# The gated unit's candidate left in PSUM in an eight-unit block pipeline, with every step placed anew

## The reference

```python
x = x + mamba(layernorm(x))        # inner 256, 16 states, 4 taps; adds its own input again
x = x + ffn(layernorm(x))          # ternary weights, 128 -> 512 -> 128, exact gelu       ("a")
x = x + gated_unit(layernorm(x))   # minGRU, 512 features
x = x + ffn(layernorm(x))          # the same ternary ffn                                   ("d")

def gated_unit(x):
    x_in, x_skip = silu(x @ W1 + b1), silu(x @ W2 + b2)
    z = sigmoid(x_in @ Wz + bz)
    h_tilde = x_in @ Wh + bh
    # h[t] = (1 - z[t]) * h[t-1] + z[t] * h_tilde[t]
    h = associative_scan(combine, (1 - z, z * h_tilde))
    return (x_skip + h) @ Wo + bo
```

## Time and profile before

| | |
|---|---|
| median of three runs | 849.96 us (849.71 to 850.46) |
| the profiled execution | 846.95 us, of which span 844.40 us |
| TensorE busy | 702.1 us (83%) |
| VectorE busy | 677.2 us (80%) |
| ScalarE busy | 641.2 us (76%) |
| GpSimd busy | 588.8 us (70%) |
| granted TensorE clock, mean of the span | 0.921 of 2.4 GHz |
| state scans (line 1118), 256 | 298.2 us, mean 1206 ns |
| gated scans (line 1224), 32 | 51.8 us, mean 1636 ns |
| candidates (line 1216), 32 | 21.5 us, mean 670 ns |

### The profile page before, as it was taken

One profiled execution on the slowest core, in us unless ns is written; L12 is line 12 of the kernel. 1 busy time (PEld: TensorE's weight loads), 2 busy tenths in 40 slices (PEclk: granted clock), 3 DMA queues, 4 the chain that ended last, 5 costly groups with the idle time before them and its releaser, 6 DMA issues. The chain is left out here.

```text
span 844.4 us, 12621 instructions
## 1 busy us (share of the span) xinstructions
PE 702.1 (83%) x4116; PEld 593.8 (70%) x4116; DVE 677.2 (80%) x1063; ACT 641.2 (76%) x968; POOL 588.8 (70%) x375
## 2 busy tenths in 40 slices
PE   5655576799788997899789979899799968997995
PEld 5444365588677886688667867688678957786795
DVE  5699988889987998899987998899779988652131
ACT  5787867796889879997899778988898578525403
POOL 4399868777778687878786877968786667515302
PEclk9677776999899999999999999999899989997999
DMA  5511212111112211121111211121111111000000
GB/s 135 180 61 56 73 52 63 52 48 54 38 53 58 68 38 50 40 77 51 50 40 63 63 39 52 43 71 38 50 43 62 49 50 38 1 1 2 13 1 12
DMA packets 35185, 42.79 MB, mean 51 GB/s; under 512 B 7457, under 2 KB 17074, under 8 KB 35122
## 3 DMA queue, kind: packets, MB, share of 16 engines
q1 hardware_dynamic: 35122, 42.00, 16.4%
HBM read 39.63 MB, written 2.36 MB: 50 GB/s over the span
## 5 line engine op out<-in xcount | busy, mean ns | idle before, releaser
L514 POOL TENSOR_TENSOR inflow<-dtu,b_all 128x1024 f32<-128x1024 f32 x127 | 307.9, 2430 | 62.2 <-DVE state L1118 43.8
L1118 DVE TENSOR_TENSOR_SCAN state<-dA,inflow 128x512 f32<-128x512 f32 x256 | 298.2, 1206 | 24.0 <-ACT dA L865 23.7
L865 ACT ACTIVATE dA<-dt,decay_c 128x512 f32<-128x512 f32 x256 | 170.0, 686 | 62.3 <-DVE state L1118 61.2
L1135 DVE TENSOR_TENSOR state<-state,c_ps 128x1024 f32<-128x1024 f32 x128 | 155.4, 1214 | 18.1 <-PE c_ps L1425 13.5
L1434 PE MATMUL y_ps<-ident,state 128*128 128x128 f32 x1024 | 148.1, 293 | 0.0
L1434 PEld LDWEIGHTS y_ps<-ident,state 128*128 128x128 f32 x1024 | 132.4, 152 | 13.2 <-issue 2.7
L1425 PE MATMUL c_ps<-xd,pick 128*128 128x512 f32 x128 | 63.1, 493 | 77.4 <-DVE state L1135 77.1
L1316 PE MATMUL work<-in_hi,wzh_hi 128*128 128x512 f32 x256 | 104.5, 408 | 0.2 <-POOL in_lo L676 0.2
L1317 PE MATMUL work<-in_hi,wzh_lo 128*128 128x512 f32 x256 | 101.0, 395 | 0.0
L1318 PE MATMUL work<-in_lo,wzh_hi 128*128 128x512 f32 x256 | 101.0, 394 | 0.0
L1425 PEld LDWEIGHTS c_ps<-xd,pick 128*128 128x128 f32 x128 | 25.4, 199 | 97.8 <-DVE state L1135 93.3
(11 more groups left out here) (171 smaller groups left out, 1506.2 us busy)
## 6 DMA issues: line engine op xcount, KB each, us to landing
b_all<-b_scratch SPq DMA_DIRECT2D x128, 256.0 KB, 3.1
x_tok<-in_x SPq DMA_DIRECT2D x8, 256.0 KB, 3.8
out_x<-x_tok SPq DMA_DIRECT2D x8, 256.0 KB, 3.6
wide<-in_Wz SPq DMA_DIRECT2D x1, 1024.0 KB, 7.7
wide<-in_Wh SPq DMA_DIRECT2D x1, 1024.0 KB, 8.8
skip_f<-in_W SPq DMA_DIRECT2D x2, 256.0 KB, 4.3
dtu<-in_W_in SPq DMA_DIRECT2D x1, 256.0 KB
mixed<-in_w_up SPq DMA_DIRECT2D x1, 256.0 KB, 2.8
```

Of the source, the lines that this page charges most:

```text
L514: eng.tensor_tensor(inflow[:, n % 2, :, tok(b)], dtu[:, :, tok(b)], b_all[:, n % RING, tok(b)].unsqueeze(1).broadcast_to([P, HALVES, TO[b] ...
L865: act.activation(dA[:, h, tok(b)], dt[:, b % 2, h, tok(b)], ACT.Exp, scale=decay_c[:, h, n:n + 1]).then_inc(s_dA[h], 1)
L1118: dve.tensor_tensor_scan(state[:, g % 3, h, tok(b)], dA[:, h, tok(b)], inflow[:, n % 2, h, tok(b)], first, ALU.mult, ALU.add).then_inc(s_s ...
L1135: dve.tensor_tensor(state[:, g % 3, :, tok(b)], state[:, g % 3, :, tok(b)], c_ps[:, tok(b)].unsqueeze(1).broadcast_to([P, HALVES, TO[b] - ...
```

## The change

The candidate stays in the bank of `h<j>`, where it overwrites its product, and the gated scan reads it there, with `keep` from SBUF; its result goes to `mixed` as before. The bank is emptied by the scan, not by the candidate. The semaphore of the scans, `s_hid`, is gone, since `evacuated(..., "h<j>")` now says the same; the candidate gets one, `s_new`, for which the scan and ScalarE's next gate in that buffer wait. The waits for the readers of `mixed` move from the candidate to the scan.

Beside this all tables are new: the places on all four engines, `MOVED` (now for units 0 to 7), and `BANK`. Most places shift by a quarter or two of a step. The larger moves in the tables of all units are shown below; `x2b` goes from 26.75 to 32, `new2`, `hid2`, `new3` and `hid3` from 34.75, 36, 35.5 and 36.5 to one quarter, 35, and in the head `w12` from 1.25 to -9.25 and `sums` from -14.25 to -6.5. Within one quarter the list of VectorE has, for each j, `new<j>` and then `hid<j>`.

```diff
 POOL_AT = {
...
-    "d.sum1": 41.5, "d.sum2": 41.75, "d.sum3": 42, "d.rms": 42.75, "x2b": 26.75, "in_lo0": 27.25,
-    "in_lo1": 27.25, "in_lo2": 27.5, "in_lo3": 27.75, "keep0": 30, "keep1": 30.5, "keep2": 33, "keep3": 33.75,
...
+    "a.rms": 24.75, "d.sum1": 41.25, "d.sum2": 41.5, "d.sum3": 41.75, "d.rms": 42.5, "x2b": 32, "in_lo0": 27,
+    "in_lo1": 27.25, "in_lo2": 27.75, "in_lo3": 28, "keep0": 29.75, "keep1": 30.75, "keep2": 32.25, "keep3": 34,
...
 DVE_AT = {
...
-    "lo1": 19.75, "lo2": 27, "lo3": 39.75, "new0": 31, "hid0": 31.75, "new1": 33, "hid1": 34, "new2": 34.75,
-    "hid2": 36, "new3": 35.5, "hid3": 36.5, "sums": -14.25, "thr": -3, "signs0": 5.25, "signs1": 6.75,
...
+    "lo3": 39.25, "new0": 31, "hid0": 31.75, "new1": 32.5, "hid1": 32.75, "new2": 35, "hid2": 35, "new3": 35,
+    "hid3": 35, "sums": -6.5, "thr": -2, "signs0": 4.75, "signs1": 6.25, "bo_add": 2.25,
...
             def gru_keep(t, j):
 
                 evacuated(pool, t, "z%d" % j)
-                wait(pool, s_hid, FB * t + j - 1)
+                evacuated(pool, t if j >= 2 else t - 1, "h%d" % ((j + 2) % FB))
...
                 p = "z%d" % j
                 act.wait_ge(s_bzh, 2)
-                if j >= 2:
-                    evacuated(act, t, "h%d" % (j - 2))
-                else:
-                    evacuated(act, t - 1, "h%d" % (j + 2))
+                wait(act, s_new, FB * t + j - 1)
                 wait(act, s_keep, FB * t + j - 1)
...
                 p = "h%d" % j
                 full(dve, t, p)
                 evacuated(dve, t, "z%d" % j)
+                dve.scalar_tensor_tensor(bank(p)[:, tok(t)], gate[:, j % 2, tok(t)], 1.0, bank(p)[:, tok(t)],
+                                         ALU.add, ALU.mult).then_inc(s_new, 1)
+
+            def gru_scan(t, j, r, s):
+                p = "h%d" % j
+                dve.wait_ge(s_new, FB * t + j + 1)
+                dve.wait_ge(s_bzh, 2)
+                dve.wait_ge(s_keep, FB * t + j + 1)
                 read_by(dve, r, s, "out+")
                 evacuated(dve, 0, "down_t")
-                dve.scalar_tensor_tensor(mixed[:, j, tok(t)], gate[:, j % 2, tok(t)], 1.0, bank(p)[:, tok(t)],
-                                         ALU.add, ALU.mult).then_inc(*emptied(p))
-
-            def gru_scan(t, j):
-                evacuated(dve, t, "h%d" % j)
-                dve.wait_ge(s_bzh, 2)
-                dve.wait_ge(s_keep, FB * t + j + 1)
                 first = nbh_c[:, j:j + 1] if FROM[t] == 0 else mixed[:, j, FROM[t] - 1:FROM[t]]
-                dve.tensor_tensor_scan(mixed[:, j, tok(t)], keep[:, j % 2, tok(t)], mixed[:, j, tok(t)], first,
-                                       ALU.mult, ALU.add).then_inc(s_hid, 1)
+                dve.tensor_tensor_scan(mixed[:, j, tok(t)], keep[:, j % 2, tok(t)], bank(p)[:, tok(t)], first,
+                                       ALU.mult, ALU.add).then_inc(*emptied(p))
...
             def gru_out(t, k):
-                pe.wait_ge(s_hid, FB * t + k + 1)
+                evacuated(pe, t, "h%d" % k)
```

More of the change, by code:

```diff
@@ new lines @@
+    ("ACT", "z_copy1", 1): -10, ("DVE", "a.ms", 1): 24.25, ("DVE", "apply", 1): -17.25,
+    ("DVE", "d.ms", 1): 43.25, ("DVE", "d.out", 1): 43.25, ("DVE", "dtu", 1): -1.25, ("DVE", "dt", 1): -2,
+    ("DVE", "factors2", 1): 26.25, ("DVE", "factors3", 1): 38, ("DVE", "gate", 1): 16.5,
+    ("DVE", "hid0", 1): 31.5, ("DVE", "hid2", 1): 34.75, ("DVE", "hid3", 1): 36.25, ("DVE", "lo1", 1): 20,
+    ("DVE", "lo2", 1): 27.5, ("DVE", "lo3", 1): 39.75, ("DVE", "new0", 1): 30.5, ("DVE", "new1", 1): 32.25,
@@ new lines @@
+    ("DVE", "lo1", 6): 19.25, ("DVE", "lo3", 6): 42.25, ("DVE", "new1", 6): 31, ("DVE", "new3", 6): 35.75,
+    ("DVE", "norm", 6): -27.25, ("DVE", "read", 6): 0.25, ("DVE", "stats2", 6): 25.25,
[12 rows of a table added]
+    ("POOL", "base", 6): -4.75, ("POOL", "conv2", 6): -13.5, ("POOL", "conv3", 6): -11.5,
+    ("POOL", "d.rms", 6): 42.25, ("POOL", "d.sum2", 6): 41.25, ("POOL", "d.sum3", 6): 42,
+    ("POOL", "h_lo", 6): -15.25, ("POOL", "in_lo0", 6): 26.5, ("POOL", "in_lo1", 6): 26.5,
[9 rows of a table added]
+    ("ACT", "gated1", 7): 15, ("ACT", "h_tok", 7): -17.75, ("ACT", "hi1", 7): 16.25, ("ACT", "hi2", 7): 25.75,
@@ L232 @@
+    ("DVE", "x3", 7): 43.25, ("DVE", "xd_lo", 7): -5.5, ("PE", "a.down+", 7): 22.5, ("PE", "a.down", 7): 22.25,
[15 rows of a table added]
+    ("POOL", "base", 7): -2.25, ("POOL", "conv2", 7): -12.5, ("POOL", "conv3", 7): -12.25,
+    ("POOL", "d.rms", 7): 47.5, ("POOL", "d.sum1", 7): 46, ("POOL", "d.sum2", 7): 46,
[3 rows of a table added]
+    ("POOL", "root", 7): -20.75, ("POOL", "x2b", 7): 41.75,
 }
@@ L1299, in _ @@
                     for t in due(r, s, DVE_ON["hid%d" % j]):
-                        gru_scan(t, j)
+                        gru_scan(t, j, r, s)
         @block.tensor
```

115 lines of the change are left out of this document (59 added, 56 removed), and 229 rows, old and new, of tables (ACT_AT, BANK, DVE_AT, MOVED).

## The result

The changed kernel takes 854.56 us (median of 5 runs, 854.28 to 854.87) against 849.96 (5 runs, 847.45 to 850.82). The ratio is 1.0054, with a 95% interval of 1.0038 to 1.0071. Forecast were 847.2 us; 854.56 lies in the range of 836 to 859, but on the other side of "no change", where the second rival (the order costs more than the stalls did, 855) had put it.

What follows compares the result with a forecast made beforehand. No engine alone was taken to bound the passes (VectorE, TensorE, ScalarE all nearly full), TensorE the tail. Terms +1.5 - 1.8 - 0.6 - 0.4 - 1.5 = -2.8 us gave 847.2 us, range 836 to 859.

Steps and rivals of the forecast that it cites:

- the second rival: Scans forced ahead of fifth state scan and norm1's transposes cost more than the stalls did: 855 us, chance 0.30.
- Part 1, the stretch goes: Gated scans on VectorE, passes of units 2 to 7: stretching vanishes, 11.5 us of VectorE time, 1.9 us a pass.
- The new scan at 1.20 us: Gated scan reading PSUM takes 1.20 us instead of 1.28, like the state scan: 2.5 us more off VectorE.
- Part 1, the mechanism: A VectorE instruction with two SBUF operands and a GpSimd one block each other; six such pairs, one per pass.
- Part 2, the candidate: Writing the 32 candidates to PSUM on VectorE costs -0.5 to +1.8 us in all; 0 taken.
- Part 3: VectorE's candidate and scan become adjacent, pairs from 4 to 19; lost overlap 0.14 us, 15 times: 2.1 us.
- Part 4: VectorE's gated scans of blocks 2 and 3 ahead of fifth state scan, units 2 to 4; with part 1: +1.5 us.
- Part 5, rden_d: GpSimd's bias add moves later, so VectorE's rden_d no longer blocks: 6.1 us freed, 1.8 us taken as arriving.
- Part 6, "passes 0 and 1 get the same work: 0": First two passes have unchanged work, so the change in their time was taken as 0.
- Part 6, the tail: TensorE's work after the last state scan, in another order: 0.6 us off, ends -3 and +3.
- The 1.5 us for GpSimd's shorter waits: GpSimd waits less for gated scans and in_lo comes earlier: -1.5 us, ends 0 and -4.
- The sign that the prediction gave for it: Passes of units 4 to 6 above 93 us would show that the order costs more.

Runs made afterwards that it cites:

- e14_units234_up1: Changed kernel with signs1/split12 later, blocks 2 and 3 of units 2 to 4 re-placed (hid3 behind fifth state scan), unit 5's a.up1 at 20.25: 848.85 us, 0.9991.
- e5_hid3_behind: Changed kernel with new2, hid2, new3, hid3 of units 2 to 4 re-placed so block 3's scan stands behind the fifth state scan: 855.70 us, 1.0068.
- e13s_units23_signs: Changed kernel with signs1 and split12 later, and block 3's scan behind the fifth state scan in units 2 and 3 only: 849.02 us, 0.9987.
- e3_signs_moved: Changed kernel with signs1 on VectorE moved from 6.25 to 6.75 and split12 on GpSimd from 7.25 to 8.25: 853.06 us, 1.0033.
- e10_block1_behind: Changed kernel with block 1 of units 2 to 4 back at its old place (new1 33, hid1 34), z3, h3, gate3 moved for the bank: 856.48 us, 1.0075.
- e15_psum_blocks23: Kernel before with hid2 at 35.5, hid3 at 36, and the candidate in PSUM for blocks 2 and 3 alone: 863.96 us, 1.0158.
- e1c_block1_only: Kernel before with only hid1 of units 0 to 5 moved from 34 to 33: 868.26 us, 1.0214.
- e2_sbuf_new_tables: Changed kernel with all its tables, but the old data path (candidate in SBUF, scan reads it there): 869.76 us, 1.0229.
- e1b_order_only: Kernel before, candidate and scan in SBUF, with only VectorE's places moved as the bank would force them: 870.69 us, 1.0250.
- e1_psum_old_tables: Kernel before with VectorE's places moved as the bank would force them, plus the change's four code hunks (candidate in PSUM): 867.27 us, 1.0201.

## Why the prediction was wrong, step by step

- **Part 1, the stretch goes: right. The new scan at 1.20 us: wrong**, it is 1.28 as before. The prediction took the state scan as its model and overlooked that it starts from an immediate (0.0, in `mix_scan`) and the gated scan from a column, which makes up 0.060 of the 0.08 us. The 2.5 us from this did not come, nor did the 2.1 us of the page's rule: by the Trainium skill, "VectorE: DVE Perf Modes", the section on the TRN2 errata, a PSUM source costs 120 cycles of fixed cost and an SBUF source 58, an estimate of 65 ns more for the new scan. The medians are 1277 from SBUF and 1279 from PSUM.
- **Part 1, the mechanism: right.** A VectorE instruction with two SBUF operands is stretched beside GpSimd's work, 3.02 us for 1.28 and 2.27 for 0.16; with one operand in PSUM, the 32 gated scans and the 8 extra ones of each of two kernels never are. It is also what the Trainium skill states in "SBUF — State Buffer", section "Who interferes with whom" (the two share a pair of ports, which is held exclusively for a whole instruction). `m_vv` and `rden_d` (up to 1.88 and 2.35 us) show it for an instruction of one SBUF operand and constants too, the signs' comparison for one with a column in SBUF beside it. The prediction used this only for the instructions that it knew to be stretched. It never asked on which ones GpSimd's work would fall in the new order.
- **Part 2, the candidate: right**, 688 ns against 662, 0.8 us in all, inside its bounds.
- **Part 3:** in the trace the adjacent pairs go from 5 to 19, not from 4, which changes the term by 0.1 us. Candidate and scan stand 0.71 and 0.70 us apart (395.14 and 397.05 above), where 0.72 was taken.
- **Part 4 is the step that failed, by its size.** It took 1.3 us more in each of three passes, and 0.8 us less in each of three others: +1.5. In the profiles the passes of units 4, 5 and 6 are 4.2, 1.9 and 1.4 us longer, those of units 2, 3 and 7 change by -1.5, +0.1 and -0.6: +5.5. The second half was nearly right (-2.0 for -2.4), the first measures 7.5 for 3.9. The path that it drew is there: in the pass of unit 4 the transposes wait for the normalisation and come 1.8 us later. What it had no term for came on top. In the pass of unit 5 TensorE stands 2.35 us on a bank that only the scan frees, and 1.7 us come back where block 3's scan stands behind the fifth state scan. In the pass of unit 4 TensorE's clock is at 1.2 GHz for 10.2 us instead of 3.4, and the prediction counted all of TensorE's work at one speed. How much of the excess the order causes and how much the clock would have taken anyway stays open. It also left out that the bank orders block 1, ahead of the second state scan (382.31 above). In the old tables the move of that one scan costs 17.8 us, as stretches that the new scan can't have; in after its delay of 2.2 us is gone two scans later.
- **Part 5, rden_d: the mechanism right, the gain not shown.** All eight are at 0.17 us in after. The move alone changes the time by +0.8 us, with 0 inside the interval, but there the stretch did not go away, so no run says what its removal is worth.
- **Part 6, "passes 0 and 1 get the same work: 0": the second step that failed,** a term put at nothing. The same work met other work. The four instructions of the signs take 1.6, 0.8, 2.6 and 2.7 us where they took 0.5, 0.8, 0.5 and 2.4, and the first pass is 3.2 us longer (`e14_units234_up1`: 3.1 of it back). The second pass is 1.4 us longer, for which no run gives the cause.
- **Part 6, the tail:** 2.3 us shorter, within its ends of -3 and +3, though 0.6 was taken. The 1.5 us for GpSimd's shorter waits appear nowhere. ScalarE's table loads are 97 in both traces, not 95: equal, as the prediction needed.
- **The second rival came true** with almost its number (855), and its mechanism (a bank that only the scan gives back) is what the runs with the old tables show. In after itself TensorE waits for scans only 3.6 us. That the number fits is partly luck: the 3.2 us of the first pass and the shorter tail (-2.3) are in it, and the rival named neither. The sign that the prediction gave for it, passes of units 4 to 6 above 93 us, holds for two of the three (95.7, 94.7, 91.9).

What stays open: the items were tested together and alone, and they do not add up exactly. The signs alone give 1.5 us; block 3 in passes 4 and 5 gives 3.2 in the profile of `e5_hid3_behind`, 1.4 of it with the clock, and pass 6 takes it back; together they give 5.5 to 5.7. `e13s_units23_signs` is 4.0 us faster than `e3_signs_moved`, from which it differs in block 2's and block 3's places alone, but of `e14_units234_up1`, which has them too, the first four passes are already 3.9 us shorter than those of `e3_signs_moved` with the same order. So the median shows that the places pay, and not by which way. And since `e10_block1_behind` had to move z3 too, the price of block 1's new place in the kernel after has not been measured by itself.

## What to carry to other kernels

A stretched instruction is a property of what two engines do at the same moment, not of the instruction: a change that removes it and moves everything else must be priced on the new neighbours of every SBUF-only instruction, also of those four columns wide. Before an intermediate result is left in a PSUM bank, count who is next in that bank and what stands behind that product on TensorE: in `e15_psum_blocks23`, where TensorE's order had not been made for it, TensorE waited 13.3 us and the kernel took 13.9 us longer. And where a data path and a whole plan change together, run each with the other's old half; +19.8 and -15.2 us looked like +4.6. And before a pass of one profile is compared with that of another, look at the granted clock: with the same lists passes differed here by up to 2.5 us.

## What the runs showed of the hardware

- A scan of 512 columns on VectorE takes 1.275 us with its start value from an SBUF column and 1.215 with an immediate, 0.060 us; whether its second operand is in SBUF or PSUM makes no difference that shows (medians of 1277 and 1279 ns).
- In `e1c_block1_only` a VectorE instruction of 128x4 elements took 2.27 us beside a GpSimd product of 128x1024 that had begun 0.15 us earlier, and ended with it (401.77 and 401.76): what it lost is the rest of GpSimd's instruction.
- The gated scans are stretched by 15.8 us in `e2_sbuf_new_tables`, and 15.2 us of time go with it. Between `e1b_order_only` and `e1_psum_old_tables` 19.2 us go away and 3.4 arrive, while TensorE's waits for banks grow by 15.7: a saving on one engine says little before the waits that the same change adds are counted.
- TensorE's granted clock differed between executions of the same lists: a pass with 504 products took 93.61 us at 0.96 and 96.15 at 0.93, TensorE being busy for 82.53 and 85.39 us.
